# A selective-scan block with a gate: eight states' inputs by diagonal matmuls, two more states moved to TensorE, small work moved between engines

## The chip, the cores and the metric

The kernel runs on one core of one Trainium2 chip. The metric is the time of the whole program on the device in microseconds (us). Four compute engines work side by side, each through its own list of instructions in order: TensorE (PE in the profile, its weight loads PEld), VectorE (DVE), ScalarE (ACT) and GpSimd (POOL). SyncE (SP) issues the DMAs. Engines wait for each other through semaphores.

## The reference, cut to what matters

```python
xn = layernorm(x)                                   # x: 32 rows x 512 tokens x 256 channels
# selective scan, forward (g=0) and backward (g=1), 16 states each:
delta = softplus(dt(xn));  B, C = projections(xn)
h[s,t] = exp(delta*A[s]) * h[s,t-1] + delta*B[s]*xn     # for each state s
y = sum_s h[s]*C[s] + D*xn                          # both directions added
# gate: one expert of eight is chosen for each row
out = gelu(xn @ W1 + b1) @ W2 ...@ Wo + biases
result = x + y * silu(xn + 0.3*out)
```

## The kernel before, in words

A loop goes over the 32 rows of the batch. Inside a row there are 32 steps, one for each state: 0 to 15 are the forward states, 16 to 31 the backward ones. A tile of a state has 128 channels on the partitions and 2 x 512 elements (two halves of the channels, all tokens). One step works as follows:

- VectorE runs one scan instruction for the state (`scan`, L861), from a decay tile and an input tile, into `hs`.
- ScalarE makes the decay tile by two Exp activations (`make_decay`, L682). It runs two states ahead.
- The input tile (delta times B times xn) is made in one of two ways. For most states GpSimd multiplies `dx` by a B row spread over the partitions by a DMA (`times_b`, L480). For the states in `TURNED` the multiplication is done with tokens on the partitions, where B of a state is one number per partition: ScalarE scales four chunks `dxT` of 128 x 256 by it (`scale_dx`, L594), and TensorE turns the result back by eight 128 x 128 transposes (`turn_bx`, L1066) into one of two PSUM slots (`dps`). In that case the decay tile lies in SBUF, else it lies in the PSUM slot. So a PSUM slot of state s comes free when the scan of state s-2 is done.
- The scan's result is multiplied by C, on GpSimd for the states in `POOL_C` (`times_c`, L468, four steps later), else on VectorE (L840), after TensorE has spread the C row over the partitions (`broadcast_c`, L1074).
- TensorE adds the product into the sum over states, by eight transposing matmuls with the identity (`add_state`, L1091): in step s for VectorE's products, in step s+2 for GpSimd's.

Around that, each engine does its part of the gate and of the next row's preparation ("front"), in steps that are written out by hand in tables (`SHIFT`, `GATE`, `FFN_OUT`, `PROJECT` and so on; a number of 32 or more is a step of the row itself, reduced by 32, a smaller one a step of the row before). All this front work goes through one PSUM bank, `fps`. The ones that matter here: TensorE's output product of the gate (`ffn_out`, L1035 and L1037) in steps 31, 0, 2 and 3; `gate_input` (L815, VectorE, steps 3 and 6), which forms 0.3 times the product plus xn; mean and variance (VectorE, step 0), their logarithm and root (ScalarE, step 1), one Newton step on 1/sqrt (`shift_of`, GpSimd, four instructions in step 6); `normalise` (ScalarE, step 6); the transposes of xn (TensorE, steps 6 and 7); the projections (TensorE, steps 8 and 9); `high_part` (ScalarE, step 11, two copies) and `low_part` (VectorE, step 12).

The order of TensorE's work within a step is fixed: the C row of state s+1, the turn of state s+3, the skip terms (`SKIP`, L1081, plain float32 matmuls of 128 x 128), the sums, then the front work. In ScalarE's step 11 the order is: the two copies of `high_part`, the decay of state 13, then a scaling if one is listed.

Of the kernel before, what the change touches and what calls it, by code (L numbers as in the profile page):

```python
# [5 lines left out]
def mamba_moe_block(nc, x, xw_f, dtw_f, dtb_f, alog_f, d_f, xw_b, dtw_b, dtb_b, alog_b, d_b,  # L6
# [62 lines left out]
    with ctx:  # L69
# [356 lines left out]
        def _(pool):  # L426
# [62 lines left out]
            def shift_of(row):  # L489

                wait_alone(pool, s_sqr, row * 3 + 3)
                wait(pool, s_xn, row * C)
                G = nc.gpsimd
                G.tensor_tensor(nwt[:, :], rsq[:, :], nvar[:, :], ALU.mult).then_inc(s_nwt, 1)
                wait_alone(pool, s_nwt, row * 3 + 1)
                G.tensor_scalar(nwt[:, :], nwt[:, :], 1.5, None, ALU.add).then_inc(s_nwt, 1)
                pool.wait_ge(s_nwt, row * 3 + 2)
                G.tensor_tensor(rs[:, :], nwt[:, :], rs[:, :], ALU.mult).then_inc(s_nwt, 1)
                pool.wait_ge(s_nwt, row * 3 + 3)
                G.tensor_tensor(shift[:, :], nmean[:, :], rs[:, :], ALU.mult).then_inc(s_shift, 1)  # L500
# [742 lines left out]
```

## Time and profile before

| | |
|---|---|
| median of 3 runs | 3112.79 us (3112.57 to 3116.84) |
| the profiled execution | 3118.2 us, its span 3116.4 us |
| busy, share of the span | DVE 97%, POOL 97%, ACT 94%, PE 80%, PEld 63% |
| mean granted TensorE clock | 0.958 |
| DMA engines, mean busy share over the row from 1501.11 us | 0.43 |

The span is about 83 us of preparation and first steps and then rows that follow each other at a nearly constant distance. Busy shares tell which engines have little room over the whole span. They do not tell which of them a given step waits for; for that the order of instructions in one row is needed.

### The profile page before, as it was taken

What the parts mean: (1) busy time and instruction counts of PE and PEld (TensorE: products, weight loads), DVE (VectorE), ACT (ScalarE), POOL (GpSimd) and SP (SyncE); (2) the same over time, 40 slices, a digit from 0 to 9 for tenths busy, and PEclk for the clock granted to TensorE, in tenths of its full rate; (3) what the DMA queues carried; (4) which work ended last, traced back from release to release, by engine and by line L of the source; (5) the groups of instructions that cost most, each with busy time, mean ns of one, the idle gap of its engine ahead of it and who ended that gap; (6) DMA issues with size and microseconds to landing.
All of it is one profiled execution on the core that took longest, in us unless ns stands there. A gap on an engine that the chain in (4) does not pass through costs nothing. (4 is left out here: it accounts for less than half of the span.)

```text
span 3116.4 us, 49216 instructions
## 1 busy us (share of the span) xinstructions
PE 2489.1 (80%) x15990; PEld 1970.9 (63%) x15990; DVE 3021.6 (97%) x1995; ACT 2940.6 (94%) x5242; POOL 3013.3 (97%) x1486
## 2 busy tenths in 40 slices
PE   7878878878778888788787788887788887887886
PEld 6666656666656666566666566666666665666665
DVE  3999999999999999999999999999999999999999
ACT  5899999999999999999999999999999999999995
POOL 3899999999999999999999999999999999999997
PEclk9999999999999999999999999999999999999998
DMA  5543334444334444344433444443444433444331
GB/s 174 151 134 116 125 119 130 143 125 119 118 123 141 135 124 123 111 131 143 130 120 119 127 128 140 127 124 111 128 139 134 126 120 114 131 144 130 107 122 55
DMA packets 273364, 394.17 MB, mean 126 GB/s; under 512 B 45003, under 2 KB 119508, under 8 KB 273108
## 3 DMA queue, kind: packets, MB, share of 16 engines
q1 hardware_dynamic: 273108, 391.03, 41.1%
q8 instruction: 127, 2.08, 0.3%
q14 instruction: 129, 1.06, 0.1%
HBM read 348.98 MB, written 25.18 MB: 120 GB/s over the span
## 5 line engine op out<-in xcount | busy, mean ns | idle before, releaser
L480 POOL TENSOR_TENSOR bx<-dx,b_sb 128x1024 f32<-128x1024 f32 x576 | 1362.9, 2388 | 10.2 <-DVE hs L861 9.5
L861 DVE TENSOR_TENSOR_SCAN hs<-decay,bx 128x1024 f32<-128x1024 f32 x576 | 1308.7, 2277 | 8.7 <-ACT decay L682 4.3
L468 POOL TENSOR_TENSOR hc<-hs,c_sb 128x1024 f32<-128x1024 f32 x480 | 1135.7, 2376 | 22.6 <-DVE hs L861 21.1
L1091 PE MATMUL y<-ident,hc 128*128 128x128 f32 x8192 | 1068.6, 277 | 36.0 <-DVE hc L840 36.0
L1091 PEld LDWEIGHTS y<-ident,hc 128*128 128x128 f32 x8192 | 942.0, 143 | 148.5 <-DVE hc L840 106.0
L861 DVE TENSOR_TENSOR_SCAN hs<-decay_sb,decay 128x1024 f32<-128x1024 f32 x448 | 1004.7, 2266 | 11.8 <-issue 10.5
L682 ACT ACTIVATE decay<-delta,rate 128x512 f32<-128x512 f32 x1152 | 745.6, 684 | 38.8 <-DVE hs L861 35.9
L594 ACT ACTIVATE dxb<-dxT,btok 128x256 f32<-128x256 f32 x1792 | 759.2, 503 | 0.3 <-PE decay L1066 0.3
L1066 PE MATMUL decay<-ident,dxb 128*128 128x128 f32 x3584 | 477.2, 276 | 244.9 <-DVE hs L861 212.8
L840 DVE TENSOR_TENSOR hc<-hs,c 128x1024 f32<-128x1024 f32 x544 | 649.6, 1194 | 1.3 <-issue 0.7
L1066 PEld LDWEIGHTS decay<-ident,dxb 128*128 128x128 f32 x3584 | 396.5, 141 | 401.3 <-issue 259.1
L682 ACT ACTIVATE decay_sb<-delta,rate 128x512 f32<-128x512 f32 x896 | 588.8, 716 | 0.1
L1074 PE MATMUL c<-dbc,selector 128*128 128x512 f32 x544 | 271.5, 499 | 204.3 <-DVE hc L840 204.3
L1035 PE MATMUL front<-w2o_sb,hT 128*128 128x256 f32 x1024 | 297.2, 442 | 39.0 <-issue 39.0
L1019 PE MATMUL front<-xnT,w_sb 128*128 128x512 f32 x512 | 244.2, 599 | 41.6 <-ACT delta L607 41.6
L1074 PEld LDWEIGHTS c<-dbc,selector 128*128 128x128 f32 x544 | 105.7, 194 | 257.8 <-DVE hc L840 248.1
L1035 PEld LDWEIGHTS front<-w2o_sb,hT 128*128 128x128 f32 x1024 | 217.8, 224 | 79.9 <-issue 48.1
L455 POOL TENSOR_TENSOR lg<-lg,ex 128x1024 f32<-128x1024 f32 x64 | 152.1, 2377 | 34.7 <-ACT lg L624 34.4
L1019 PEld LDWEIGHTS front<-xnT,w_sb 128*128 128x128 f32 x512 | 87.3, 190 | 116.5 <-issue 61.2
L460 POOL TENSOR_TENSOR delta<-lg,delta 128x1024 f32<-128x1024 f32 x64 | 152.7, 2386 | 0.1
L445 POOL TENSOR_TENSOR dx<-delta,xnT 128x1024 f32<-128x1024 f32 x64 | 152.1, 2377 | 0.1
L584 ACT ACTIVATE dxT<-front 128x512 f32<-128x512 f32 x128 | 75.0, 586 | 33.5 <-PE front L995 33.5
(125 smaller groups left out, 2050.8 us busy)
## 6 DMA issues: line engine op xcount, KB each, us to landing
b_sb<-b_scratch SPq DMA_DIRECT2D x576, 256.0 KB, 3.3
c_sb<-b_scratch SPq DMA_DIRECT2D x480, 256.0 KB, 3.5
xin<-in_L_attn_x_dram SPq DMA_DIRECT2D x32, 512.0 KB, 6.6
w_sb<-in_L_ffn_W_dram SPq DMA_DIRECT2D x32, 512.0 KB, 3.4
w2o_sb<-w2o_scratch SPq DMA_DIRECT2D x32, 512.0 KB
xres<-in_L_attn_x_dram SPq DMA_DIRECT2D x32, 512.0 KB, 5.4
out_dram<-og SPq DMA_DIRECT2D x32, 512.0 KB, 4.3
dbc<-high SPq DMA_DIRECT2D x64, 128.0 KB, 2.3
```

What stands on the lines that cost most here:

```text
L460: nc.gpsimd.tensor_tensor(delta[:, g * (1 + par), :, :], lg[:, :, :], delta[:, g * (1 + par), :, :], ALU.add).then_inc(s_delta, 1)
L468: nc.gpsimd.tensor_tensor(hc[:, s % RING, :, :], hs[:, s % HSLOTS, :, :], c_sb[:, i % CRING, :].unsqueeze(1).broadcast_to([P, DT, T]), ALU ...
L480: nc.gpsimd.tensor_tensor(bx[:, i % RING, :, :], dx[:, g, :, :], b_sb[:, i % BRING, :].unsqueeze(1).broadcast_to([P, DT, T]), ALU.mult).th ...
L594: A(dxb[:, (row * NT + i) % XSLOTS, c, :], dxT[:, g, c, :], ACT.Copy, scale=btok[:, par, c, g, n:n + 1]).then_inc(s_dxb, 1)
L682: return A(to[:, k, :], delta[:, g * (1 + par), k, :], ACT.Exp, scale=rate[:, g, k, n:n + 1])
L840: V.tensor_tensor(hc[:, s % RING, :, :], hs[:, s % HSLOTS, :, :], cps[:, :].unsqueeze(1).broadcast_to([P, DT, T]), ALU.mult).then_inc(s_hc, 1)
L861: V.tensor_tensor_scan(hs[:, s % HSLOTS, :, :].rearrange("p k t -> p (k t)")[:, u], factor.rearrange("p k t -> p (k t)")[:, u], data.rearr ...
L1019: ins = M(fps[:, :], w1_sb[:, k, j * P:(j + 1) * P], xnT[:, par, k, :], start=(k == 0), stop=(k == DT - 1))
L1035: M(to, hT[:, j, c * P:(c + 1) * P], w2o_sb[:, j, :], start=(j == 0), stop=False)
L1066: ins = nc.tensor.transpose(dps[s % DSLOTS][:, k, c * P:(c + 1) * P], dxb[:, (row * NT + i) % XSLOTS, c, k * P:(k + 1) * P], ident[:, :])
L1074: M(cps[:, :], selector[:, N + n:N + n + 1].broadcast_to([P, P]), dbc[:, par, g, :], start=True, stop=True).then_inc(s_cps, 1)
L1091: ins = M(yps[:, c, k * P:(k + 1) * P], hc[:, s % RING, k, c * P:(c + 1) * P], ident[:, :], start=False, stop=(s == ADDED[-1]), is_transpo ...
```

## The change

1. For the states 5, 6, 8, 9, 10, 11, 12, 13 (`DIAGONAL`) ScalarE scales the 128 x 128 identity by B instead of the 128 x 256 chunk of `dxT`. TensorE then multiplies the unscaled chunk with this diagonal matrix, by eight plain float32 matmuls instead of eight transposes.
2. States 10 and 12 are made in this way too; before, GpSimd made their input tiles. The steps at which ScalarE scales are set anew: the full scaling of state 14 and state 15 are at steps 10 and 11 now (9 and 10 before).
3. The product with C of state 8 moves from VectorE to GpSimd (and its C row from TensorE to a DMA).
4. `gate_input`: the factor 0.3 is folded into the expert's weights in the preparation, xn is added on TensorE by one more float32 matmul with the identity for each chunk of 128 tokens, and a ScalarE copy replaces the VectorE instruction.
5. The Newton step moves from GpSimd in step 6 to VectorE in step 3, in three instructions instead of four, and ScalarE makes no negative mean for it.
6. One B buffer fewer (5), one buffer of scaled tiles more (4). The copy of `dxT` waits until the turns that read it are done.

The constants:

```diff
-    BRING, CRING, C_AHEAD = 6, 5, 3
-    TSLOTS, XSLOTS = 3, 3
-
-    MEAN, SCALE, SHIFT, NORM = 0, 1, 6, 6
+    BRING, CRING, C_AHEAD = 5, 5, 3
+    TSLOTS, XSLOTS = 3, 4
+
+    MEAN, SCALE, SHIFT, NORM = 0, 1, 3, 6
...
-    TURNED, SCALED_AT, TURN_LEAD = (5, 6, 8, 9, 11, 13, 14, 15, 22, 24, 26, 28, 29, 30), (1, 2, 3, 4, 5, 7, 9, 10, 17, 19, 21, 23, 24, 25), 3
+    TURNED, SCALED_AT, TURN_LEAD = (5, 6, 8, 9, 10, 11, 12, 13, 14, 15, 22, 24, 26, 28, 29, 30), (1, 2, 3, 4, 5, 7, 8, 9, 10, 11, 17, 19, 21, 23, 24, 25), 3
     POOL_B = [s for s in range(STEPS) if s not in TURNED]
-    POOL_C, C_LAG, ADD_LAG = (2, 4, 5, 7, 9, 10, 11, 12, 16, 18, 20, 22, 24, 26, 27), 4, 2
+    POOL_C, C_LAG, ADD_LAG = (2, 4, 5, 7, 8, 9, 10, 11, 12, 16, 18, 20, 22, 24, 26, 27), 4, 2
     ON_DVE = [s for s in range(STEPS) if s not in POOL_C]
+    DIAGONAL = (5, 6, 8, 9, 10, 11, 12, 13)
```

ScalarE (the copy of `dxT`, the scaling, the gate's copy; the Identity activation that made `nmean` is gone):

```diff
             def copy_dxT(row, i):
                 g, half = i // 2, i % 2
+                wait(act, s_bxT, (row - 1) * NT + (FIRST_TURNED[1] if g == 0 else NT))
...
                 for c in range(C):
-                    A(dxb[:, (row * NT + i) % XSLOTS, c, :], dxT[:, g, c, :], ACT.Copy, scale=btok[:, par, c, g, n:n + 1]).then_inc(s_dxb, 1)
+                    if TURNED[i] in DIAGONAL:
+                        A(dxb[:, (row * NT + i) % XSLOTS, c, 0:P], ident[:, :], ACT.Copy, scale=btok[:, par, c, g, n:n + 1]).then_inc(s_dxb, 1)
+                    else:
+                        A(dxb[:, (row * NT + i) % XSLOTS, c, :], dxT[:, g, c, :], ACT.Copy, scale=btok[:, par, c, g, n:n + 1]).then_inc(s_dxb, 1)
...
+            def gate_input(row, v):
+                act.wait_ge(s_pf, row * UNITS + 12 + v)
+                if v == 0:
+                    wait(act, s_yg, row)
+                A(zz[:, 2 * v:2 * v + 2, :], fps[:, :].rearrange("p (c d) -> p c d", c=2), ACT.Copy).then_inc(s_zz, 1)
```

VectorE (`shift_of` is called at step 3 after the scan and the product with C; GpSimd's four-instruction version is gone):

```diff
+            def shift_of(row):
+                dve.wait_ge(s_sqr, row * 2 + 2)
+                wait(dve, s_xn, row * C)
+                V.tensor_tensor(nwt[:, :], rsq[:, :], nvar[:, :], ALU.mult).then_inc(s_nwt, 1)
+                dve.wait_ge(s_nwt, row * 2 + 1)
+                V.scalar_tensor_tensor(rs[:, :], nwt[:, :], 1.5, rs[:, :], ALU.add, ALU.mult).then_inc(s_nwt, 1)
+                dve.wait_ge(s_nwt, row * 2 + 2)
+                V.scalar_tensor_tensor(shift[:, :], mv[:, :, 0], -1.0, rs[:, :], ALU.mult, ALU.mult).then_inc(s_shift, 1)
...
-            def gate_input(row, v):
-                dve.wait_ge(s_pf, row * UNITS + 12 + v)
-                if v == 0:
-                    wait(dve, s_yg, row)
-                V.scalar_tensor_tensor(zz[:, 2 * v:2 * v + 2, :], fps[:, :].rearrange("p (c d) -> p c d", c=2), 0.3,
-                                       xn[:, 2 * v:2 * v + 2, :], ALU.mult, ALU.add).then_inc(s_zz, 1)
```

TensorE:

```diff
                 if half:
-                    ins = M(to, ones3[:, :], bias3[:, :], start=False, stop=True)
+                    M(to, ones3[:, :], bias3[:, :], start=False, stop=False)
+                    ins = M(to, ident[:, :], xn[:, c, :], start=False, stop=True)
...
+                slot = (row * NT + i) % XSLOTS
                 for k in range(DT):
                     for c in range(C):
-                        ins = nc.tensor.transpose(dps[s % DSLOTS][:, k, c * P:(c + 1) * P],
-                                                  dxb[:, (row * NT + i) % XSLOTS, c, k * P:(k + 1) * P], ident[:, :])
+                        if s in DIAGONAL:
+                            ins = M(dps[s % DSLOTS][:, k, c * P:(c + 1) * P], dxT[:, s // N, c, k * P:(k + 1) * P],
+                                    dxb[:, slot, c, 0:P], start=True, stop=True)
+                        else:
+                            ins = nc.tensor.transpose(dps[s % DSLOTS][:, k, c * P:(c + 1) * P],
+                                                      dxb[:, slot, c, k * P:(k + 1) * P], ident[:, :])
```

In the preparation, ScalarE's copies of the multiplied weights (L677) get the factor 0.3, and VectorE multiplies the bias row by 0.3 in one more small instruction.

## Rows read from the trace of the kernel before

**Rows 1.** Stretches: length, busy us of PE, PEld, DVE, ACT, POOL; PEclk, DMA, GB/s.
```profile
1501.11:1595.48 94.37, 75.91 (x493) 60.17 (x493) 93.76 (x62) 91.29 (x164) 93.46 (x47) 0.97 0.43 127
...
1504.37:1507.73 3.36, 3.36 (x8) 2.49 (x9) 3.36 (x4) 3.35 (x5) 3.36 (x3) 0.56 0.69 222
...
1528.00:1538.10 10.10, 7.51 (x53) 5.58 (x52) 9.74 (x6) 9.76 (x21) 10.10 (x6) 1.00 0.47 101
```
**Rows 2.** Instructions grouped by line: counts, busy us, mean ns | idle before, releaser.
```profile
L468 POOL TENSOR_TENSOR hc<-hs,c_sb 128x1024 f32<-128x1024 f32 x480 | 1135.7, 2376 | 22.6 <-DVE hs L861 21.1
...
L1066 PE MATMUL decay<-ident,dxb 128*128 128x128 f32 x3584 | 477.2, 276 | 244.9 <-DVE hs L861 212.8 <-ACT dxb L594 32.2
L1035 PE MATMUL front<-w2o_sb,hT 128*128 128x256 f32 x1024 | 297.2, 442 | 39.0 <-issue 39.0
...
L1081 PE MATMUL y<-dskip_diag,xnT 128*128 128x128 f32 x512 | 86.7, 307 | 0.0
```
**Rows 3.** Timeline of TensorE in that row: start, us, operation [idle before].
```profile
1504.37 3.43 PE L1035 MATMUL front<-w2o_sb,hT 128*128 128x256 f32 x8 [0.63 <-issue]
1507.73 0.28 PE L1037 MATMUL front<-bias,ones 3*128 3x256 bf16 x1
1507.94 0.50 PE L1074 MATMUL c<-dbc,selector 128*128 128x512 f32 x1
1508.28 0.60 PE L1081 MATMUL y<-dskip_diag,xnT 128*128 128x128 f32 x4
1508.72 1.04 PE L1091 MATMUL y<-ident,hc 128*128 128x128 f32 x8
1509.59 1.89 PE L1035 MATMUL front<-w2o_sb,hT 128*128 128x256 f32 x8
1511.42 0.28 PE L1037 MATMUL front<-bias,ones 3*128 3x256 bf16 x1
1511.63 1.16 PE L1081 MATMUL y<-dskip_diag,xnT 128*128 128x128 f32 x8
...
1524.15 1.06 PE L1066 MATMUL decay<-ident,dxb 128*128 128x128 f32 x8 [0.99 <-DVE hs L861]
...
1529.63 1.06 PE L1066 MATMUL decay<-ident,dxb 128*128 128x128 f32 x8 [0.69 <-DVE hs L861]
...
1535.12 1.06 PE L1066 MATMUL decay<-ident,dxb 128*128 128x128 f32 x8 [0.78 <-ACT dxb L594]
```
**Rows 4.** Timeline of VectorE in that row.
```profile
1512.88 0.67 DVE L815 SCALAR_TENSOR_TENSOR zz<-front,xn 128x512 f32<-128x512 f32 x1
1513.46 2.28 DVE L861 TENSOR_TENSOR_SCAN hs<-decay,bx 128x1024 f32<-128x1024 f32 x1
1515.66 1.19 DVE L840 TENSOR_TENSOR hc<-hs,c 128x1024 f32<-128x1024 f32 x1
1516.77 4.46 DVE L861 TENSOR_TENSOR_SCAN hs<-decay_sb,decay 128x1024 f32<-128x1024 f32 x2
...
1525.04 4.45 DVE L861 TENSOR_TENSOR_SCAN hs<-decay_sb,decay 128x1024 f32<-128x1024 f32 x2
...
1538.10 4.47 DVE L861 TENSOR_TENSOR_SCAN hs<-decay_sb,decay 128x1024 f32<-128x1024 f32 x2 [0.36 <-issue]
```
**Rows 5.** Timeline of ScalarE in that row.
```profile
1516.10 1.70 ACT L594 ACTIVATE dxb<-dxT,btok 128x256 f32<-128x256 f32 x4
1517.70 1.32 ACT L682 ACTIVATE decay_sb<-delta,rate 128x512 f32<-128x512 f32 x2
...
1536.21 0.58 ACT L574 ACTIVATE projected<-front 128x512 f32<-128x512 f32 x1
1536.69 2.55 ACT L682 ACTIVATE decay_sb<-delta,rate 128x512 f32<-128x512 f32 x4
```
**Rows 6.** Who waited for whom, over the whole span: us, times, longest.
```profile
DVE zz L815 <- PE front L1037: 12.8, 24, 3.3
DVE hs L861 <- issue: 11.3, 30, 0.8
```

More of the change, by code:

```diff
@@ L59, in mamba_moe_block @@
     AHEAD, AHEAD_NEXT = {5: 8, 14: 22, 15: 24, 16: 26, 23: 28, 26: 29, 27: 30}, {29: 5}
-    EPS = 1e-5
+    EPS, FFN_SCALE = 1e-5, 0.3
     LN_SCALE, LN_SHIFT = 0.6110144853591919, 0.6499999761581421
@@ L126, in mamba_moe_block @@
         nvar = sb("nvar", [P, C])
-        nmean = sb("nmean", [P, C])
         rsq = sb("rsq", [P, C])
@@ L164, in mamba_moe_block @@
         wo_sb = decay_sb[:, 1, 1, :].rearrange("p (k n) -> p k n", k=DT)
-        bo_row, bias_rest, bias_rest2 = dxb[0:1, 0, 0, :], dxb[0:NE, 0, 1, :], dxb[0:NE, 0, 2, :]
+        bo_row, bias_rest, bias_rest2, bias_sum = dxb[0:1, 0, 0, :], dxb[0:NE, 0, 1, :], dxb[0:NE, 0, 2, :], dxb[0:NE, 0, 3, :]
         w2_in = (w2o_sb, xres)
@@ L202, in mamba_moe_block @@
         s_bias, s_biasc, s_biasst, s_b2T, s_dtz = (sem(n) for n in ("bias_ready", "bias_parts", "bias_stored", "b2T_loaded", "dtw_zeroed"))
+        s_biass = sem("bias_scaled")
         s_proj, s_bstored = sem("projected_copied"), sem("b_stored")
@@ L487, in residual @@
                 nc.gpsimd.tensor_tensor(og[:, :, :], og[:, :, :], xres[:, :, :], ALU.add).then_inc(s_out, 1)
[L489 to L500, printed above, removed]
             def front(row, par, s):
-                if s == SHIFT:
-                    shift_of(row)
                 if s in LOG1P:
@@ L512, in front @@
                     cut(row, par, CUT.index(s))
-            shift_of(0)
             log1p(0, 0)
@@ L545, in normalise_scale @@
                 A(nvar[:, :], mv[:, :, 1], ACT.Identity, scale=-0.5, bias=half_eps[:, :]).then_inc(s_sqr, 1)
-                A(nmean[:, :], mv[:, :, 0], ACT.Identity, scale=-1.0).then_inc(s_sqr, 1)
                 act.wait_ge(s_ln, row + 1)
@@ L653, in drain @@
                     hidden(row, HIDDEN.index(s))
+                at = GATE if row else GATE_FIRST
+                if s in at:
+                    gate_input(row, at.index(s))
             def front(row, par, s):
@@ L677, in copy_w2o @@
                 A(w2o_st[a][:, 2 * h:2 * h + 2, :], w2o_ps[a][h][:, :].rearrange("p (j d) -> p j d", j=2),
-                  ACT.Copy).then_inc(s_w2oc, 1)
+                  ACT.Copy, scale=FFN_SCALE).then_inc(s_w2oc, 1)
             def decay_of(row, par, s, to, k):
@@ L797, in mean_variance @@
                 dve.wait_ge(s_x, row * 16 + 16)
-                wait(dve, s_shift, row)
                 for c in range(C):
@@ L820, in front @@
                     mean_variance(row)
+                if s == SHIFT:
+                    shift_of(row)
                 if s == LOW:
                     low_part(row)
-                at = GATE if row else GATE_FIRST
-                if s in at:
-                    gate_input(row, at.index(s))
             def output(row):
@@ L873, in _ @@
             dve.wait_ge(s_xwT, 1)
+            shift_of(0)
             V.tensor_copy(wx[:, :, :], wx_ps[:, 0:2 * P].rearrange("p (k m) -> p k m", k=DT)).then_inc(s_wev, 1)
@@ L918, in _ @@
             dve.wait_ge(s_bias, 1)
-            bias_sum = bias_ps[0:NE, 0:D]
+            V.tensor_scalar(bias_sum, bias_ps[0:NE, 0:D], FFN_SCALE, None, ALU.mult).then_inc(s_biass, 1)
+            dve.wait_ge(s_biass, 1)
             V.tensor_copy(bias_part[:, 0, :], bias_sum).then_inc(s_biasc, 1)
             dve.wait_ge(s_biasc, 1)
-            V.tensor_tensor(bias_rest[:, :], bias_sum, bias_part[:, 0, :], ALU.subtract).then_inc(s_biasc, 1)
+            V.tensor_tensor(bias_rest[:, :], bias_sum[:, :], bias_part[:, 0, :], ALU.subtract).then_inc(s_biasc, 1)
             dve.wait_ge(s_biasc, 2)
```

## The prediction

> **What bounds the kernel now.** I read the page's busy shares first: DVE and POOL 97%, ACT 94%, PE 80% of the span. Then the busy time by stretches of one row, to see whether the last engines are equally full everywhere; then the groups of instructions, for counts and durations; then, and mostly, the timelines of TensorE, VectorE and ScalarE through one row, since in a pipeline as tight as this only the order inside a row says what a longer instruction list costs.
>
> The row from 1501.11 us lasts 94.37 us, and VectorE is busy for 93.76 of them, GpSimd for 93.46, ScalarE for 91.29, TensorE for 75.91 [rows 1]. So VectorE sets the pace. Its only named wait that returns in every row is 0.36 us ahead of the scan of state 13 [rows 4], 11.3 us in 30 waits over the span [rows 6]; there ScalarE's decay of state 13 ends last, which stands behind the two copies of `high_part`. The other wait is for the gate's product, 12.8 us in 24 waits [rows 6].
>
> TensorE looks as if it had 20% to spare. The timeline shows where that room is. From 1504.37 us, when the gate's activation allows it to start on the gate's output product, it works almost without a pause: first at half clock (0.56 is granted, the eight instructions take 3.43 us and not 1.89) and then at full clock [rows 1, 3]. Up to its turn of state 13 at 1535.12 us it has three pauses of note, 0.99, 0.69 and 0.78 us, together 2.5 us [rows 3], or 2.9 if each is counted from when the next instruction could have been started. The rest of its idle time lies later in the row. **All that the change adds to TensorE lies in this first third.**
>
> **The price of the edits on TensorE.** A transpose of 128 x 128 is one instruction: 3584 of them are 32 rows x 14 states x 8 [rows 2]. A plain float32 matmul is two: the skip terms are 8 matmuls a row and have 512 instructions over 32 rows, and the gate's 16 matmuls a row have 1024 [rows 2]. The distance from one instruction to the next is 0.11 us for both kinds at 128 columns: four of the skip terms' from 1508.28 to 1508.72, eight transposing ones from 1508.72 to 1509.59 [rows 3]. So eight transposes take 0.87 us and eight plain matmuls 16 x 0.11 = 1.76. At 256 columns four matmuls take 1.83 us (1509.59 to 1511.42), or 0.43 to 0.46 each [rows 3]. Per row:
> - six old turns (5, 6, 8, 9, 11, 13): 6 x (1.76 - 0.87) = +5.3
> - two new turns (10, 12): +3.5
> - xn added by four matmuls: +1.7
> - no C row for state 8 (1508.28 - 1507.94 = 0.34): -0.3; its sum (0.87) moves from step 8 to step 10, both within the stretch.
>
> That is +10.2 us before the turn of state 13 is finished. Against it stand the pauses (2.9) and the distance by which the turn was early: it ended at about 1536.1 us, with 0.2 us for the signal, and the scan came at 1538.10 [rows 3, 4]; 1.8 us. 10.2 - 2.9 - 1.8 = 5.5; but the sum of state 8 now comes behind the turn of 13 (-0.9), which leaves 4.6 by this crude count.
>
> **The same in order of time**, to see that the pauses can be filled and which scans wait. TensorE reaches the turn of state 5 at 1514.6 us instead of 1513.7 (two matmuls for xn), ends it at 1516.3, in time for the scan at 1516.77 [rows 4]. Then product 1.83, bias 0.20, xn 0.43: the turn of 6 runs from 1518.8 to 1520.6, and the scan of 6, due at 1518.97, starts at 1520.8: 1.8 late. Then sum 0.87, product, bias and xn 2.46, skip 0.44, sum 0.87, C row 0.32: the turn of 8 ends at 1527.3, its scan starts at 1527.5 instead of 1525.04 [rows 4]. Turn of 9 to 1529.1; two sums and four transposes of xn 2.2; turn of 10 to 1533.0; sum and transposes 1.3; turn of 11 to 1536.1; a projection 0.86 (two instructions); turn of 12 to 1538.7; sum and projection 1.7; turn of 13 from 1540.4 to 1542.2, scan at 1542.4: +4.3 us. From the turn of 6 on TensorE never waits for a scan: VectorE waits for it.
>
> ScalarE adds to this. It can copy the projection only from 1540.6 us on; two copies at 0.48 (1536.21 to 1536.69) and the decay of 13 (a pair of activations; four take 2.55 us, two 1.32, so 1.23 for a pair) bring the scan of 13 to 1542.9 [rows 5]. Behind it now stands the scaling of 15 (1.6 us, 1516.10 to 1517.70 [rows 5]) before the decay of 14, ready at about 1545.6 when VectorE is through at 1545.1. So +0.5 more: **+5.3 us a row**, which I take; 4.3 is the bound from TensorE alone.
>
> **What the other edits give.** VectorE: product with C of state 8 gone, -1.11 (1515.66 to 1516.77); two gate instructions gone, -0.58 each (1512.88 to 1513.46) [rows 4]; the Newton step is three dependent instructions on 4 elements; bounded below by nothing and above by three of the gate's, 1.7, I take 0.6. It takes the very place of the first gate instruction. These 1.7 us are already in the walk: they are what VectorE would gain if its tiles came in time. GpSimd: two B products fewer and one C product more, net -1 at 2.38 [rows 2], and the Newton step, about -3.5 us a row; it then has 9 us of room in a row of 99, so the smaller B ring, the one C load more and the two B loads fewer in SP's queue hide. ScalarE: one activation follows the other after 0.61 us at 512 columns and 0.40 at 256 [rows 5], so 0.19 fixed and 0.82 ns a column, and a scaling of 128 columns is 0.30: 32 x 0.30 + 32 x 0.40 = 22.4 us against 56 x 0.40 = 22.4. Two gate copies add 0.96, the negative mean leaves 0.1. Its gain before state 7 is lost, because the decay of 7 waits for the scan of 5; its load rises by 0.9 us. The gate's first copy finds TensorE's product finished at about 1512.6 us and comes itself at about 1512.4, a wait of some tenths ahead of a scaling that has room; the new wait of the `dxT` copy is for turns that ended many steps before; the Newton step waits for ScalarE's step 1, which the shorter scaling brings forward. The folded 0.3 and the longer bias chain cost under 1 us once.
>
> The Trainium skill, "TensorE: Matmul & The Clock Gate", Terms, says that transpose mode is four times faster for float32. By that a turn would go from 0.87 to 3.5 us, and a row would get some 14 us longer than in my sum; the trace shows plain float32 at two instructions of the same pace [rows 2, 3], so I go by 1.76.
>
> **Sum.** The full rows 1 to 30: 30 x 5.3 = 159. Row 0 has the gate's product in other steps: 4. The last row has no transposes and projections between the turns: 2.5. Where TensorE is late before already (the 24 waits for the gate [rows 6]), its delay now passes on to every later scan: 5, between 0 and 12.8. The preparation: -1, the Newton step without GpSimd. Together +169. Against the profiled execution (3118.2 us, span 3116.4) that is 3287; the median lies 5.4 lower, so 3282; I say 3280.
>
> **Rivals.** (a) TensorE's spare fifth takes it all. If a diagonal turn took no longer than transposes plus some tenths, so that it fits between two scans with the sums around it (under about 1.1 us), VectorE's 1.7 us would be the gain: 31 x 1.7 = 53, 3060. For it: PE 80% and the last row of the stretch busy 7.51 of 10.10 us [rows 1]. Against it: the counts in rows 2. 0.06. (b) ScalarE decides alone: turns in time, but the copies, the new scalings and decay of 13 and 14 in steps 5 to 12 eat VectorE's gain: within 0.4 us a row of now, about 3112. 0.03. (c) TensorE, busier, gets full clock at the row's start: the 3.36 us at 0.56 shrink by 1.5, a row +3.8, 3235. Against it: nothing is added in the pauses that precede the half clock. The Trainium skill, same page, "Part 4: PE-mode transpose", says that transposes don't count as busy for the clock gate, by which plain matmuls could raise it; but from 1528.00 the clock is 1.00 with transposes for nearly all instructions [rows 1]. 0.06. (d) ScalarE's tail is worse, because dependent decays, `dxT` copies and TensorE's front work push each other: another 1 us a row, 3311. 0.12. (e) The forecast, 3240 to 3300: 0.70. What is left, 0.03, is longer still.
>
> **Range and chances.** 3225 to 3315 holds (c), (d) and (e) but for their tails, 0.85. What a measurement of this kernel can tell from no change is 0.2%, 6 us. Faster by more: 0.06. Within: 0.03. Slower: 0.91.
>
> **What the profile of the changed kernel would show.** TensorE's turn line splits into transposes and matmuls, the latter 32 x 8 x 16 = 4096 instructions at 0.11 us from one to the next. PE about 84 to 88 us a row, in a row of 99 to 100 us; DVE's share falls to about 92%, POOL's to 92%. VectorE's scans of states 6, 8, 10, 11, 12 wait for PE's turn, 1 to 2 us each; the scans of 13 and 14 for ScalarE. TensorE has no pause between 1507 us and the turn of 13 in such a row. I would be wrong if scans in steps 6 to 12 follow each other at 2.2 us, if diagonal turns last about 1 us, or if the row's second half, which I take to be unchanged, grows or shrinks too.

## The result and the profile after

The changed kernel takes 3325.4 us (median of 4 runs, 3323.0 to 3333.9), the kernel before 3114.8 us on the same chip: a ratio of 1.068 with a 95% interval of 1.0657 to 1.0702. It is slower, as forecast, but by 211 us and not by 167: the forecast was 3280 and the top of the range 3315.

The head of the page, with the busy shares:

```profile
span 3324.4 us, 54911 instructions
...
PE 2807.0 (84%) x18774; PEld 2324.1 (70%) x18774; DVE 3086.8 (93%) x1996; ACT 2965.0 (89%) x5530; POOL 2923.4 (88%) x1326
```

VectorE is no longer filled, and TensorE, the emptiest of the four, has become 84% busy. The stretches of one row, in the columns of [rows 1]; the first line is a whole row, the second its part from the turn of state 5 to the end of the turn of state 13, the third its second half:

```profile
1393.05:1493.74 100.69, 85.60 (x580) 70.85 (x580) 96.03 (x62) 92.02 (x173) 91.01 (x42) 0.97 0.38 117
1406.52:1434.92 28.40, 28.16 (x216) 25.53 (x215) 25.14 (x14) 21.41 (x48) 20.89 (x10) 1.00 0.43 130
1445.18:1493.74 48.56, 36.41 (x234) 27.24 (x234) 48.47 (x28) 48.09 (x82) 47.18 (x22) 1.00 0.31 103
```

In the second line TensorE is busy for 28.16 of 28.40 us, where the row before still had three pauses of note [rows 3]. In the third it has 12 us to spare. The groups of instructions:

```profile
L1068 PE MATMUL decay<-dxb,dxT 128*128 128x128 f32 x4096 | 495.8, 276 | 3.5 <-DVE hs L858 3.5
L1071 PE MATMUL decay<-ident,dxb 128*128 128x128 f32 x2048 | 275.6, 279 | 120.5 <-DVE hs L858 115.0 <-ACT dxb L582 5.4
L580 ACT ACTIVATE dxb<-ident,btok 128x128 f32<-128x128 f32 x1024 | 323.7, 388 | 0.0
L805 DVE TENSOR_TENSOR nwt<-rsq,nvar 128x4 f32<-128x4 f32 x32 | 39.5, 1235 | 1.0 <-ACT rsq L534 1.0
L807 DVE SCALAR_TENSOR_TENSOR rs<-nwt,rs 128x4 f32<-128x4 f32 x32 | 71.2, 2225 | 1.1
L809 DVE SCALAR_TENSOR_TENSOR shift<-mv,rs 128x4 f32<-128x4 f32 x32 | 7.3, 228 | 1.1
```

The turns have split as forecast, into 4096 matmul instructions and 2048 transposes, and TensorE has almost nothing to wait for ahead of the first kind (3.5 us in the whole span). The last three lines are the Newton step, for which the forecast had 0.6 us in all: two of its VectorE instructions on four elements last 1235 and 2225 ns on the mean. The timeline of VectorE through the same row shows them in their place:

```profile
1402.62 2.28 DVE L858 TENSOR_TENSOR_SCAN hs<-decay,bx 128x1024 f32<-128x1024 f32 x1
1404.82 1.55 DVE L805 TENSOR_TENSOR nwt<-rsq,nvar 128x4 f32<-128x4 f32 x1
1406.41 2.28 DVE L807 SCALAR_TENSOR_TENSOR rs<-nwt,rs 128x4 f32<-128x4 f32 x1
1408.73 0.16 DVE L809 SCALAR_TENSOR_TENSOR shift<-mv,rs 128x4 f32<-128x4 f32 x1
1408.84 2.29 DVE L858 TENSOR_TENSOR_SCAN hs<-decay,bx 128x1024 f32<-128x1024 f32 x1
...
1412.16 4.46 DVE L858 TENSOR_TENSOR_SCAN hs<-decay_sb,decay 128x1024 f32<-128x1024 f32 x2
...
1420.11 4.46 DVE L858 TENSOR_TENSOR_SCAN hs<-decay_sb,decay 128x1024 f32<-128x1024 f32 x2 [0.20 <-PE decay L1068]
...
1425.98 2.29 DVE L858 TENSOR_TENSOR_SCAN hs<-decay_sb,decay 128x1024 f32<-128x1024 f32 x1 [1.41 <-PE decay L1068]
...
1429.08 2.29 DVE L858 TENSOR_TENSOR_SCAN hs<-decay_sb,decay 128x1024 f32<-128x1024 f32 x1 [0.81 <-ACT decay_sb L679]
...
1435.73 2.29 DVE L858 TENSOR_TENSOR_SCAN hs<-decay_sb,decay 128x1024 f32<-128x1024 f32 x1 [0.58 <-ACT decay_sb L679]
...
1438.56 2.29 DVE L858 TENSOR_TENSOR_SCAN hs<-decay_sb,decay 128x1024 f32<-128x1024 f32 x1 [0.54 <-ACT decay_sb L679]
```

And GpSimd at the same time:

```profile
1403.99 2.36 POOL L481 TENSOR_TENSOR bx<-dx,b_sb 128x1024 f32<-128x1024 f32 x1
1406.32 2.35 POOL L461 TENSOR_TENSOR delta<-lg,delta 128x1024 f32<-128x1024 f32 x1
```

VectorE's first small instruction ends at 1406.37, 0.02 us after GpSimd's product (1406.35); the second at 1408.69, 0.02 us after GpSimd's next (1408.67). The third lies where GpSimd's list has a gap and takes 0.16 us. This is so in all rows: of the 32 executions of each of the first two, 31 begin while a GpSimd instruction runs, and every one of these ends 0.016 to 0.024 us after it. The scan of 1402.62, during which GpSimd's product begins, lasts 2.28 us, as the one of 1408.84 does, beside which GpSimd is idle.

To compare with the forecast's own steps I took the starts of all scans from both traces and averaged over the rows 2 to 29. The table gives by how many us a scan comes later than in the kernel before, counted from the row's first scan; e1, below, is the changed kernel with the Newton step back on GpSimd.

| scan of state | forecast | changed kernel | e1 |
|---|---|---|---|
| 6 | 1.8 | 3.4 | 2.3 |
| 8 | 2.5 | 3.2 | 2.8 |
| 13 | 4.8 | 5.8 | 5.3 |
| 14 | 5.3 | 6.5 | 5.9 |
| next row | 5.3 | 6.7 | 6.0 |

A mean row of the changed kernel lasts 101.4 us, of the one before 94.7.

### The profile page after: what moved, and what is told of

The parts are those of the page before. It is cut to its first block and busy times, and to the rows that moved or that the text cites. A ratio compares the mean times of both kernels' runs of the same rounds, so it can differ in the third digit from the quotient of the medians.

```text
span 3324.4 us, 54911 instructions
## 1 busy us (share of the span) xinstructions
PE 2807.0 (84%) x18774; PEld 2324.1 (70%) x18774; DVE 3086.8 (93%) x1996; ACT 2965.0 (89%) x5530; POOL 2923.4 (88%) x1326
## 5 line engine op out<-in xcount | busy, mean ns | idle before, releaser
L858 DVE TENSOR_TENSOR_SCAN hs<-decay_sb,decay 128x1024 f32<-128x1024 f32 x512 | 1157.3, 2274 | 139.6 <-PE decay L1068 67.4
L481 POOL TENSOR_TENSOR bx<-dx,b_sb 128x1024 f32<-128x1024 f32 x512 | 1208.3, 2381 | 52.1 <-PE y L1096 31.2
L858 DVE TENSOR_TENSOR_SCAN hs<-decay,bx 128x1024 f32<-128x1024 f32 x512 | 1164.2, 2279 | 9.2 <-ACT decay L679 4.7
L1096 PEld LDWEIGHTS y<-ident,hc 128*128 128x128 f32 x8192 | 944.3, 143 | 123.8 <-DVE hc L837 100.2
L679 ACT ACTIVATE decay_sb<-delta,rate 128x512 f32<-128x512 f32 x1024 | 677.1, 716 | 2.0 <-DVE hs L858 2.0
L1068 PEld LDWEIGHTS decay<-dxb,dxT 128*128 128x128 f32 x4096 | 488.4, 192 | 40.4 <-issue 29.1
L1068 PE MATMUL decay<-dxb,dxT 128*128 128x128 f32 x4096 | 495.8, 276 | 3.5 <-DVE hs L858 3.5
L582 ACT ACTIVATE dxb<-dxT,btok 128x256 f32<-128x256 f32 x1024 | 437.0, 509 | 0.0
L1071 PEld LDWEIGHTS decay<-ident,dxb 128*128 128x128 f32 x2048 | 233.0, 144 | 219.5 <-issue 136.1
L1071 PE MATMUL decay<-ident,dxb 128*128 128x128 f32 x2048 | 275.6, 279 | 120.5 <-DVE hs L858 115.0
L580 ACT ACTIVATE dxb<-ident,btok 128x128 f32<-128x128 f32 x1024 | 323.7, 388 | 0.0
L1079 PEld LDWEIGHTS c<-dbc,selector 128*128 128x128 f32 x512 | 101.4, 198 | 266.9 <-DVE hc L837 260.9
```

The source lines that it names most:

```text
L481: nc.gpsimd.tensor_tensor(bx[:, i % RING, :, :], dx[:, g, :, :], b_sb[:, i % BRING, :].unsqueeze(1).broadcast_to([P, DT, T]), ALU.mult).th ...
L679: return A(to[:, k, :], delta[:, g * (1 + par), k, :], ACT.Exp, scale=rate[:, g, k, n:n + 1])
L858: V.tensor_tensor_scan(hs[:, s % HSLOTS, :, :].rearrange("p k t -> p (k t)")[:, u], factor.rearrange("p k t -> p (k t)")[:, u], data.rearr ...
L1068: ins = M(dps[s % DSLOTS][:, k, c * P:(c + 1) * P], dxT[:, s // N, c, k * P:(k + 1) * P], dxb[:, slot, c, 0:P], start=True, stop=True)
L1071: ins = nc.tensor.transpose(dps[s % DSLOTS][:, k, c * P:(c + 1) * P], dxb[:, slot, c, k * P:(k + 1) * P], ident[:, :])
L1079: M(cps[:, :], selector[:, N + n:N + n + 1].broadcast_to([P, P]), dbc[:, par, g, :], start=True, stop=True).then_inc(s_cps, 1)
```

## The experiments

Times are medians; the ratio behind each is to the kernel before measured beside it (3117.0 for e1 to e4, 3117.3 for e5 to e8, 3116.7 for e9 to e12, 3115.8 for e13 to e15). The first question was whether the Newton step's 3.7 us are what the forecast missed, and what TensorE's part costs.

**e1: the Newton step back on GpSimd in step 6, all else as changed.**

```diff
-    MEAN, SCALE, SHIFT, NORM = 0, 1, 3, 6
+    MEAN, SCALE, SHIFT, NORM = 0, 1, 6, 6
```

(and GpSimd's `shift_of` of the kernel before.) 

> The changed kernel with the Newton step back on GpSimd in step 6. Theory T (TensorE's order binds: the two small VectorE instructions of 1 to 2.3 us in step 3 only cover a wait that the turn of state 6 would cause anyway): a row shortens by at most 0.5 us, 3305 to 3325 us in all. Rival N (the Newton step's 3.4 us a row come on top of what TensorE costs): 3325 - 31 x 3.4 = 3220 us.

Measured: 3300.8 us, ratio 1.0591 (1.0573 to 1.0608), 4 us under the range of theory T and 81 above the rival. 25 us come back (27 when each kernel is taken against the kernel before measured beside it), not the whole excess over the forecast. The list of who waited for whom says why:

```profile
DVE hs L867 <- PE decay L1076: 142.3, 153, 2.1
```

The changed kernel has this line at

```profile
DVE hs L858 <- PE decay L1068: 67.4, 97, 2.1
```

Without the small instructions VectorE comes earlier to the scan of state 6 and waits there for TensorE (4.35 us from scan 5 to scan 6, against 2.20). So most of the Newton step's time replaces a wait that was there anyway.

**e2: all turns by transposes.**

```diff
-    DIAGONAL = (5, 6, 8, 9, 10, 11, 12, 13)
+    DIAGONAL = ()
```

> The changed kernel with an empty list of diagonal states: all turned states, 10 and 12 too, by scaled dxT and transposes. Theory T: TensorE's load in the first third falls by 7 us, its waits go; what stays is the Newton step (3.4 us a row) less VectorE's gain (1.7) plus some waiting for ScalarE, which has 3.2 us more work: a row of about 97, 3200 us. If the Newton step were hidden or harmless without the diagonal matmuls: 3110 to 3150. If TensorE is not what costs: over 3290.

Measured: 3273.2 us, 1.05 (1.0483 to 1.0518): 52 us come back. That lies between the expectations of 3200 and of over 3290, and is met by neither. The Newton step now costs most of what it takes, since no TensorE wait hides it (80 us, by e8 below), and ScalarE has the full scalings of ten states in the first half. One edit undone doesn't give its price while others stand in its place.

**e3: the kernel before with the Newton step alone on VectorE in step 3.** The diff is that of `shift_of` in the section on the change. 

> The kernel before with one edit, the Newton step on VectorE in step 3. Theory P (a VectorE instruction with two SBUF inputs can't run while a GpSimd tensor-tensor instruction does, and waits for its end): GpSimd is busy all the time, so each of three instructions waits for a boundary, 3.4 us a row as in the changed kernel, less 0.4 for a wait that it covers: 3115 + 31 x 3 = 3208 us. Rival Q (small instructions cost 0.15 us each as in the preparation): 3115 + 31 x 0.6 = 3134 at most.

Measured: 3213.1 us, 1.0313 (1.0296 to 1.033), 5 us from what was expected. The step from scan 3 to scan 4 is 6.23 us on the mean and 2.86 before. Its timeline, with GpSimd's instructions between:

```profile
1554.35 2.37 POOL L479 TENSOR_TENSOR bx<-dx,b_sb 128x1024 f32<-128x1024 f32 x1
1555.77 0.97 DVE L790 TENSOR_TENSOR nwt<-rsq,nvar 128x4 f32<-128x4 f32 x1
1556.68 2.36 POOL L459 TENSOR_TENSOR delta<-lg,delta 128x1024 f32<-128x1024 f32 x1
1556.78 2.30 DVE L792 SCALAR_TENSOR_TENSOR rs<-nwt,rs 128x4 f32<-128x4 f32 x1
1559.11 0.16 DVE L794 SCALAR_TENSOR_TENSOR shift<-mv,rs 128x4 f32<-128x4 f32 x1
```

Again VectorE's ends follow GpSimd's by 0.02 to 0.04 us in the times as printed. These three instructions on four elements cost the kernel before 96 us.

**e4: as e3, but each of the three reads one tile.**

```diff
-                V.tensor_tensor(nwt[:, :], rsq[:, :], nvar[:, :], ALU.mult).then_inc(s_nwt, 1)
+                V.tensor_scalar(nwt[:, :], nvar[:, :], 1.0, None, ALU.mult).then_inc(s_nwt, 1)
...
-                V.scalar_tensor_tensor(rs[:, :], nwt[:, :], 1.5, rs[:, :], ALU.add, ALU.mult).then_inc(s_nwt, 1)
+                V.tensor_scalar(rs[:, :], rs[:, :], 1.0, None, ALU.mult).then_inc(s_nwt, 1)
```

(and the third likewise.) 

> As e3_newton_alone, but each of the three instructions reads one SBUF tile only (a tensor_scalar with a constant), at the same place, with the same waits and writes; the Newton correction and the product mean times 1/sqrt are left out of the computation. Theory P: each takes about 0.15 us whatever GpSimd does, 3115 + 31 x 0.5 = about 3120 to 3130 us. Rival (the delay comes from the place, from the wait for ScalarE or from three dependent instructions, not from the second input): as e3_newton_alone, 3200 or more.

Measured: 3219.0 us, 1.033 (1.0313 to 1.0347). A miss: nothing comes back.

```profile
L790 DVE TENSOR_SCALAR nwt<-nvar 128x4 f32<-128x4 f32 x32 | 30.5, 953 | 1.0 <-ACT rsq L533 1.0
L792 DVE TENSOR_SCALAR rs<-rs 128x4 f32<-128x4 f32 x32 | 71.2, 2224 | 1.1
```

The durations are those of the forms with two inputs. So it isn't the second input alone that makes VectorE wait; this run left open whether every small VectorE instruction in this place would wait.

**e5: as e3, but the three are bn_aggr, which reads one tile too.**

```diff
-                V.tensor_tensor(nwt[:, :], rsq[:, :], nvar[:, :], ALU.mult).then_inc(s_nwt, 1)
+                V.bn_aggr(nwt[:, 0:2], stats[:, 0, :]).then_inc(s_nwt, 1)
...
-                V.scalar_tensor_tensor(rs[:, :], nwt[:, :], 1.5, rs[:, :], ALU.add, ALU.mult).then_inc(s_nwt, 1)
+                V.bn_aggr(nwt[:, 2:4], stats[:, 1, :]).then_inc(s_nwt, 1)
```

(and the third likewise.) 

> As e3_newton_alone, but the three instructions are bn_aggr on 128 x 6 statistics, the operation that takes 0.16 us in step 0 while GpSimd is busy; one SBUF input and no tensor_scalar. The Newton step is left out of the computation and the shift is filled with a variance. Theory P2 (two-input SBUF instructions and plain tensor_scalar or copy forms wait for GpSimd's running instruction, others don't): three times 0.16 us, a row 0.1 to 0.5 us longer, 3115 to 3132 us. Rival (any small VectorE instruction in step 3 waits for GpSimd, or the place and its three dependent waits cost 3 us): 3205 or more.

Measured: 3141.4 us, 1.0076 (1.0059 to 1.0093): 72 us less than e3, but 9 above the range. The step from scan 3 to scan 4 is 0.5 us longer than before, as expected; the rest comes mostly in the second half of the row, where the step of scan 28 is 0.5 us longer and VectorE's list has 14 waits for a turn (13.9 us in all).

```profile
L793 DVE BATCH_NORM_AGGREGATE nwt<-stats 128x2 f32<-128x6 f32 x32 | 5.8, 182 | 1.1
```

Same place, same chain of three, same GpSimd beside it: 182 ns instead of 2225, and 31 of the 32 executions of each lie wholly within a running GpSimd instruction. With e3 and e4 this shows the cause: whether the form of instruction waits for a running GpSimd instruction. The Trainium skill, "SBUF — State Buffer", § Who interferes with whom, says that VectorE and GpSimd share a pair of ports which one instruction holds to its end, that VectorE needs it for an instruction with two SBUF inputs, and also for copies and tensor_scalar in a fast mode that uses both ports. The durations of e3 and e5 agree with it; those of e4 (953 and 2224 ns) do if its tensor_scalar ran in that mode, which no run shows.

**e6: the kernel before with diagonal turns for its own six states.**

```diff
+    DIAGONAL = (5, 6, 8, 9, 11, 13)
```

(and the branches of `scale_dx` and `turn_bx`.) 

> The kernel before with one edit, the diagonal matmuls for the six of its turned states among 5 to 13 (5, 6, 8, 9, 11, 13). TensorE gets 5.3 us more in the first third, against pauses of 2.9 us and 1.2 to 1.9 us by which turns are early. Theory T: scans of 6 and 8 wait 0.8 us together, the wait of the scan of 13 for ScalarE (0.4) goes: 3120 to 3150 us. Rival (each diagonal turn's 0.9 us counts in full, 5.3 a row): 3280. Rival (ScalarE's 2.4 us less make the row shorter): under 3108.

Measured: 3210.4 us, 1.0297 (1.028 to 1.0314). A miss, 60 us above the range. VectorE's row shows two waits, for the turn of state 6 and then for the gate's product:

```profile
1566.16 2.29 DVE L866 TENSOR_TENSOR_SCAN hs<-decay_sb,decay 128x1024 f32<-128x1024 f32 x1 [1.63 <-PE decay L1073]
...
1568.97 0.69 DVE L820 SCALAR_TENSOR_TENSOR zz<-front,xn 128x512 f32<-128x512 f32 x1 [0.53 <-PE front L1042]
```

The gate's second half stands on VectorE behind the scan of 6; ScalarE's `normalise` waits for it (69.4 us in 31 waits over the span), and behind that stand the transposes of xn, the projections and the decay of 13. A delay at the turn of 6 thus travels down the row through all engines. My expectation had given the turns the pauses of the best row and no such chain.

**e7: the kernel before with the gate's change alone** (factor in the weights, xn on TensorE, copies on ScalarE). 

> The kernel before with one edit, the gate's sum on TensorE and its copy on ScalarE. VectorE has 1.16 us a row less, TensorE 1.7 and ScalarE 0.96 more, both ahead of the scan of 13, where ScalarE is late already. Theory T: 3108 to 3140 us, no gain. Rival (VectorE's gain counts in full): 3115 - 31 x 1.1 = 3080.

Measured: 3141.7 us, 1.008 (1.0063 to 1.0098), 2 us above the range. VectorE is spared two instructions of 0.58 us in every row, and yet 24 us are lost. VectorE's waits show where: for the turn of state 6, ahead of which every unit of the gate's product has two matmul instructions more, and for the C row that TensorE spreads. The kernel before has one wait of each kind in the whole span (0.7 and 0.6 us):

```profile
DVE hs L861 <- PE decay L1068: 26.6, 32, 0.8
DVE hc L840 <- PE c L1076: 20.0, 33, 1.3
```

**e8: the changed kernel without diagonal turns and with the Newton step on GpSimd** (the edits of e1 and e2 together). 

> The changed kernel with neither the diagonal matmuls nor the Newton step on VectorE: states 10 and 12 turned by transposes, state 8's product on GpSimd, the gate on TensorE and ScalarE. ScalarE has 3.2 us more in steps 5 to 11 than before. Theory T: scans of 13 and 14 wait for ScalarE, row 96.4, 3150 to 3180 us. Rival (the 2.3 us that VectorE is spared come out): 3045.

Measured: 3193.0 us, 1.0237 (1.022 to 1.0255), 13 us above the range. So even what is left of the change, the gate, states 10 and 12 turned, the scalings' new steps, the buffers and C of state 8 on GpSimd, costs 76 us. (This run and e2 differ by the Newton step alone: 80 us.)

**e9: e1, but the turn of a diagonal state is eight transposes of the scaled identity.** ScalarE's shorter scaling stays, TensorE's instruction count falls to that of transposes.

```diff
-                            ins = M(dps[s % DSLOTS][:, k, c * P:(c + 1) * P], dxT[:, s // N, c, k * P:(k + 1) * P],
-                                    dxb[:, slot, c, 0:P], start=True, stop=True)
+                            ins = nc.tensor.transpose(dps[s % DSLOTS][:, k, c * P:(c + 1) * P],
+                                                      dxb[:, slot, c, 0:P], ident[:, :])
```

> e1_newton_back with eight transposes of the scaled identity in place of the eight diagonal matmuls of a state: the same operands scaled by ScalarE, the same waits, half the instructions on TensorE. The input tiles of the eight states then hold the scaled identity and not the product with dxT, so that part of the computation is left out. Theory T (TensorE's 7.1 us a row for 64 more instructions is what binds): most of e1_newton_back's excess goes, a row of 94.8 to 96, 3115 to 3160 us. Rival (ScalarE's order, the moved product or the gate's copy bind): over 3230.

Measured: 3182.2 us, 1.0213 (1.0198 to 1.0229); above the range by 22 us, far under the rival's. It differs from e1 by TensorE's turns alone, so 118 us are the price of the doubled instructions there. The group of these turns, with TensorE's own waits ahead of them:

```profile
L1076 PE MATMUL decay<-ident,dxb 128*128 128x128 f32 x2048 | 261.3, 273 | 2.2 <-ACT dxb L599 1.4 <-DVE hs L867 0.6 <-ACT dxb L597 0.2
```

2048 instructions for what were 4096 (L1068 above). Against e8 it has the shorter scalings alone: 10 us better (the two intervals overlap a little, so the size is rough). That is all that the change's main idea gives back when it costs TensorE nothing.

**e10: e6 with the buffers of the change** (`BRING` 5, `XSLOTS` 4). 

> e6_diag_six with the rings of the changed kernel (4 buffers of scaled tiles, 5 of B). In e6_diag_six ScalarE waited 60 us in all for a scaled tile's buffer. If that ring costs: 3150 to 3185 us. If TensorE alone binds there: 3200 to 3212, no change.

Measured: 3206.6 us, 1.0298 (1.0282 to 1.0313), as e6. The buffers play no part there.

**e13: the kernel before with states 10 and 12 turned by transposes and C of state 8 on GpSimd, alone** (the lines of `TURNED`, `SCALED_AT`, `POOL_C` and the buffers). 

> The kernel before with states 10 and 12 turned by transposes and state 8's product on GpSimd, nothing else. If the parts add up (e8_neither is 76 us over before, the gate alone 24): 3117 + 52 = 3169, between 3155 and 3180, by waits for ScalarE's decays of 13 and 14. If the two don't add up (one wait covers the other): 3130 or 3190.

Measured: 3175.2 us, 1.0193 (1.0177 to 1.0209), as expected. ScalarE has ten full scalings in the first half, and VectorE waits for its decays three times a row, where before only the scan of 13 did [rows 6]:

```profile
DVE hs L861 <- ACT decay_sb L682: 51.7, 93, 0.6
```

The last four runs asked whether the same idea pays in the second half of the row, where TensorE has 12 us to spare.

**e11: diagonal turns in the second half, state 25 turned, C of 23 on GpSimd; the first half as before.** (The buffers are those of the change, here and in e12, e14 and e15.)

```diff
+    DIAGONAL = (22, 24, 25, 26, 28, 30)
-    POOL_C, C_LAG, ADD_LAG = (2, 4, 5, 7, 9, 10, 11, 12, 16, 18, 20, 22, 24, 26, 27), 4, 2
+    POOL_C, C_LAG, ADD_LAG = (2, 4, 5, 7, 9, 10, 11, 12, 16, 18, 20, 22, 23, 24, 26, 27), 4, 2
```

> The kernel before with diagonal matmuls where TensorE has its pauses, in the second half of the row (22, 24, 25, 26, 28, 30), with state 25 turned in addition and state 23's product on GpSimd instead. VectorE has 1.1 us a row less, GpSimd the same, ScalarE 1.2 less, TensorE 6.2 more of its 12 us idle there. Theory T (only the place on TensorE matters): the row gets shorter by 0.3 to 0.9 us, 3088 to 3107 us. Rival (diagonal matmuls cost wherever they stand): over 3125.

Measured: 3158.0 us, 1.0132 (1.0116 to 1.0147). A miss. The scan of state 26 waits for its turn, 65 us in 32 waits:

```profile
DVE hs L866 <- PE decay L1073: 65.1, 32, 2.1
```

**e12: as e11, state 20 turned too.** 

> As e11_second_one with state 20 turned as well (diagonal too): GpSimd 2.3 us a row less, ScalarE as before, TensorE 8 us more in the second half. Theory T: VectorE's 1.1 us come out in full if ScalarE keeps up, 3080 to 3105. Rival (TensorE or ScalarE bind in the second half): 3120 or more.

 Measured: 3217.4 us, 1.0321 (1.0307 to 1.0335), a miss: 108 us of waits for turns, in 64 waits.

**e14: as e11, with 22 and 24 alone diagonal.** 

> e11_second_one with diagonal matmuls for 22 and 24 only; 25, 26, 28 and 30 by transposes. If the length of the turns of 25 and 26 made the wait of 2.1 us ahead of the scan of 26: it falls to 0.3, a row of 94.1 to 94.6, 3095 to 3112 us. If ScalarE (0.8 us a row more than before) binds: 3115 to 3135.

 Measured: 3168.5 us, 1.0173 (1.0159 to 1.0187), a miss. The waits for TensorE's turns are smaller (27.2 us for 77.9 in e11), another has come, for GpSimd, which has three products with C in a row (22, 23, 24). It had them in e11 too, where VectorE came later and did not wait for them:

```profile
DVE hs L866 <- POOL hc L469: 38.2, 43, 1.1
```

**e15: as e11, none diagonal.** 

> e11_second_one with no diagonal state: ScalarE has 1.6 us a row more than before, TensorE 0.9, VectorE 1.1 less. If TensorE's order alone matters: 3085 to 3105 us. If ScalarE's load in the second half binds (it has some 0.5 us of pauses there): 3120 to 3150.

 Measured: 3191.8 us, 1.0248 (1.0234 to 1.0262), a miss: waits for ScalarE's decays (31.2 us), for GpSimd (41.1) and for TensorE (21.2). Against e15 the diagonal turns of e11 do win 34 us, but the second half as it was remains the best that I found.

## Why the forecast was right in direction and too low in size

**What held.** VectorE set the pace before. A plain float32 turn is 16 instructions at 0.11 us: in TensorE's timeline of the changed kernel one starts at 1406.52 and the next work at 1408.30, 1.78 us for the 1.76 forecast.

```profile
1406.52 1.95 PE L1068 MATMUL decay<-dxb,dxT 128*128 128x128 f32 x16
1408.30 1.89 PE L1034 MATMUL front<-w2o_sb,hT 128*128 128x256 f32 x8
1410.13 0.28 PE L1036 MATMUL front<-bias,ones 3*128 3x256 bf16 x1
1410.34 0.70 PE L1037 MATMUL front<-xn,ident 128*128 128x256 f32 x2
1411.27 2.02 PE L1068 MATMUL decay<-dxb,dxT 128*128 128x128 f32 x16 [0.24 <-DVE hs L858]
```

The pauses between filled up, in order of the forecast's walk; from the turn of 8 on the scans wait for TensorE (those of 8, 10 and 12 in the row shown), those of 13 and 14 for ScalarE (that of 11 does so too, which the walk had put down to TensorE). TensorE is busy for 85.60 us of the row, forecast 84 to 88; VectorE's share is 93% (forecast 92), GpSimd's 88% (forecast 92, harmless, since no scan waits for it in this row). The second half of the row shown is unchanged in time (48.56 us; the row before from 1546.90 us had 48.58, and TensorE is busy for 36.41 in both). The rivals (a) to (c) fall by the time measured. On (a), e1 and e9 show that TensorE's spare fifth did not take the doubled instructions, they cost 118 us; on (c), the half clock at the row's start is still there (0.50 granted, below).

**What failed first: the Newton step's term.** I had taken 0.6 us for three instructions on four elements, bounded above by three of the gate's, 1.7. They take 3.7 us together. The bound came from VectorE instructions of another kind: the gate's read one of their two inputs from PSUM. The mechanism that was missing is the wait for a running GpSimd instruction, which e3, e4 and e5 show. It costs 96 us where VectorE sets the pace (e3). In the changed kernel it is worth 27 us (to e1) of the 43 by which the loss of 210.6 us exceeds the forecast one of 167: it stands ahead of a wait for TensorE and mostly replaces it. So the scan of 6, which the forecast let wait 1.8 us, doesn't wait in the row shown, and is later still: 3.4 us in the table's mean.

How these 27 us come about differs from row to row, and it shows a second thing that the walk had wrong: "From the turn of 6 on TensorE never waits for a scan". In 8 of the rows 2 to 29, those in which TensorE gets through the first two units of the gate's product soonest, the turn of 6 waits for the PSUM slot that the late scan of 4 frees (by 0.16 to 0.27 us; the one at 1411.27 above is such a wait), and it does so in no other row from 2 to 29. These rows last 100.7 us, those of e1 that begin equally soon 100.2. In the other 20 rows the scan of 8 comes 15.9 us behind TensorE's second bias matmul in both kernels, so there the small instructions hold nothing up directly. On the mean over all rows this direct part is 0.13 us of the 0.74 by which the changed kernel's row is longer than e1's. 0.3 us more come from TensorE's second bias matmul, which is later, and 0.24 from the second half; in both places TensorE ran at half clock in rows shown below. Why the half clock costs more with the Newton step on VectorE, no run shows.

**What failed second: small terms of the walk.** In e1, where the Newton step stands as before, every scan from 6 on is still 0.3 to 0.6 us later than the walk had it, and the row 0.7 longer. The loss of e1 is 183.9 us, 17 above the forecast one. The walk began from the row at 1501.11 us, one of the shortest (the rows before last from 94.37 to 95.48 us), so the rows with a late start are the first suspects. I measured in all rows how long it is from the start of the gate's activation to TensorE's second bias matmul: 9.06 us in that row, 9.8 on the mean over the rows before, 9.95 in e1 and 10.3 in the changed kernel, the last two with one pair of xn's matmuls more in it (0.35 us). In e1 every second row starts as early as the walk's row. One of them, with VectorE's first instruction of the row ahead:

```profile
1585.37 1.40 DVE L816 BATCH_NORM_STATS2 stats<-xin 128x6 f32<-128x256 f32 x4
...
1602.63 0.70 PE L1045 MATMUL front<-xn,ident 128*128 128x256 f32 x2
1603.16 1.95 PE L1076 MATMUL decay<-dxb,dxT 128*128 128x128 f32 x16
1605.15 2.29 DVE L867 TENSOR_TENSOR_SCAN hs<-decay_sb,decay 128x1024 f32<-128x1024 f32 x1 [2.07 <-PE decay L1076]
...
1624.95 1.95 PE L1076 MATMUL decay<-dxb,dxT 128*128 128x128 f32 x16
1627.54 2.29 DVE L867 TENSOR_TENSOR_SCAN hs<-decay_sb,decay 128x1024 f32<-128x1024 f32 x1 [0.58 <-ACT decay_sb L696]
1630.36 2.29 DVE L867 TENSOR_TENSOR_SCAN hs<-decay_sb,decay 128x1024 f32<-128x1024 f32 x1 [0.53 <-ACT decay_sb L696]
```

| us after the row's start | walk | this row |
|---|---|---|
| turn of 6 begins | 17.7 | 17.8 |
| scan of 6 | 19.7 | 19.8 |
| turn of 13 begins | 39.3 | 39.6 |
| scan of 13 | 41.8 | 42.2 |
| scan of 14 | 44.5 | 45.0 |
| next row | 99.7 | 100.2 |

So the walk is 0.5 us short with its own start. The pair of matmuls for xn takes 0.53 us (1602.63 to 1603.16) where it had 0.43, a turn 1.78 and not 1.76; from the beginning of the turn of 13 to the scan it is 2.6 us and not 2.5, from there to the scan of 14 2.8 and not 2.7. Each is a rounding. With no pause left they add up, to 15 us over 30 rows, which is most of the 17. Late starts are not it: the mean row of e1 is 0.50 us above its shortest, that of the kernel before 0.36, a difference of 4 us over 30 rows, for which the forecast had 5.

In the changed kernel the mean row is 0.74 us above the shortest, so late starts and the second half add 11 us there to what they cost before. In its row from 1593 us TensorE starts the gate's product at 1597.98, and half clock lasts until 1604.18 (the second line has the columns of [rows 1]):

```profile
1597.98 3.75 PE L1034 MATMUL front<-w2o_sb,hT 128*128 128x256 f32 x8 [1.75 <-issue]
1601.66:1604.18 2.52, 2.52 (x10) 2.02 (x9) 2.06 (x2) 2.49 (x11) 1.97 (x2) 0.52 0.09 28
```

In [rows 3] the eight instructions took 3.43 us after a pause of 0.63, and the sum at 1508.72 already had its full pace.

The part in the second half is new and stands in single rows: the step of scan 28 is 0.2 us longer on the mean (2.40 for 2.18), because in some rows half clock falls on the turns there too, and eight transposes take 1.91 us instead of 1.04:

```profile
1682.28 1.91 PE L1071 MATMUL decay<-ident,dxb 128*128 128x128 f32 x8
1682.28:1684.19 1.91, 1.91 (x10) 1.91 (x9) 0.95 (x1) 1.82 (x4) 1.91 (x2) 0.50 0.00 0
1684.23 2.29 DVE L858 TENSOR_TENSOR_SCAN hs<-decay_sb,decay 128x1024 f32<-128x1024 f32 x1 [0.99 <-PE decay L1071]
```

Rival (d) had said another 1 us a row and 3311, by ScalarE's tail. The size was near (1.4 us a row); the cause, but for the 0.2 us at the scans of 13 and 14, wasn't that.

**Where the 211 us come from.** Each line is the difference of two runs, each against the kernel before measured beside it:

| | us |
|---|---|
| Newton step on VectorE (changed kernel, +210.6, less e1, +183.9) | 27 |
| doubled TensorE instructions (e1, +183.9, less e9, +65.6) | 118 |
| the rest: gate, states 10 and 12, C of 8, with short scalings (e9) | 66 |

These shares hold for this order of undoing alone. With the Newton step left in place, the diagonal turns are worth 54 us and not 118 (the changed kernel less e2), since VectorE's later coming then takes the place of much of the waiting that they cause; without the diagonal turns the Newton step is worth 80 (e2 less e8).

The rest can be split only roughly: the gate alone costs 24 (e7), the turns and C of 8 alone 59 (e13), together 83 or, measured, 76 (e8); the shorter scalings give 10 back. The gate's edit costs its 24 us ahead of the turn of 6 (e7); whether its matmuls or its ScalarE copy do it, no run separates. And none of the edits that were run, alone or in a part, made the kernel faster, although each takes work from an engine that was 94 to 97% busy.

## What to carry to other kernels

When the pace-setting engine is 97% busy and its suppliers are early by only a microsecond or two, price an edit by the order inside a row, and keep the hundredths of every term: a chain that fills its last pause passes on every delay it used to absorb, and a handful of small roundings made 0.5 us a row here. Check in all rows, not in one, whether the row that you walk is a typical one. A small VectorE instruction is not free beside a busy GpSimd: ask from where it reads and what GpSimd runs at that moment, and if it must be moved, put it ahead of a wait (27 us here and not 96), or give it a form that doesn't wait (e5). To have ScalarE scale less by having TensorE multiply more in float32 costs two instructions for one; it gave ScalarE time worth 10 us here and took 118.

## What the runs showed of the hardware that was not expected

- A VectorE instruction on 128 x 4 elements with inputs in SBUF lasted to the end of the GpSimd instruction beside it, to within 0.04 us in all 31 rows in which there was one (e3, e4 and the changed kernel): 2225 ns on the mean, 160 ns in a gap of GpSimd's. tensor_tensor, scalar_tensor_tensor and a float32 tensor_scalar did so; bn_aggr on 6 elements (182 ns) and the scans, one input of which lies in PSUM (2.28 us with GpSimd and without), didn't.
- The granted TensorE clock was half at a row's start (0.56 from 1504.37 us before, 0.50 and 0.52 from 1597.98 us after), for a stretch that differs from row to row: the way from the gate's activation to the second bias matmul took 9.0 to 10.45 us in the kernel before. In some rows it was half for turns of the second half too (0.50 from 1682.28 us). The mean over the span was 0.956 (0.958 before) although TensorE was busy for 84% of the span and not 80%.
